# Reordering the operations of a pair on four engines, with carry and floor moved to ScalarE

## What is computed

```python
xn = _layernorm(x, axis=-1)
x = x + attn(xn, ...) + ffn(xn, ...)
...
# ffn: six layers (DEPTH = 6, HEADS = 16, DIM_HEAD = 64, WINDOW = 32)
for i in range(DEPTH):
    x = attn_layer(shift_tokens(x), Wqkv[i], ...) + x
    x = ffn_layer(shift_tokens(x), ...) + x
...
# attn_layer
q = l2norm(q) * qs
k = l2norm(k) * ksc
q = q * cos * scale + rotate_half(q) * sin * scale
k = k * cos * inv + rotate_half(k) * sin * inv
out = local_attention(q, k, v)   # each window of 32 sees itself and the window before
return out @ Wo
...
# ffn_layer
xn = (x - mu) / jnp.sqrt(var + 1e-05) * g + bln
a, gate = jnp.split(xn @ W1 + b1, 2, -1)
return a * jax.nn.gelu(gate, approximate=False) @ W2 + b2
```

## Time and profile before

| what | value |
|---|---|
| runs before | 3851.44, 3864.42, 3864.74 us, median 3864.42 |
| profiled execution | 3854.79 us, its span 3853.0 us |
| granted TensorE clock, mean | 0.984 |
| TensorE busy | 3672.5 us (95%) |
| VectorE busy | 3196.5 us (83%) |
| ScalarE busy | 2919.4 us (76%) |
| GpSimd busy | 3063.6 us (80%) |

### The profile page before, as it was taken

One profiled execution on the slowest core, in us unless ns is written; L12 is line 12 of the kernel. 1 busy time (PEld: TensorE's weight loads), 2 busy tenths in 40 slices (PEclk: granted clock), 3 DMA queues, 4 the chain that ended last, 5 costly groups with the idle time before them and its releaser, 6 DMA issues. The chain is left out here.

```text
span 3853.0 us, 176449 instructions
## 1 busy us (share of the span) xinstructions
PE 3672.5 (95%) x66944; PEld 2523.9 (66%) x66944; DVE 3196.5 (83%) x6391; ACT 2919.4 (76%) x6003; POOL 3063.6 (80%) x3927
## 2 busy tenths in 40 slices
PE   4999997899999999999999999999999999999997
PEld 2344443567777777777777777777777777777775
DVE  6888884788888888888888888888888888888885
ACT  6466666677777887778777777787778777778874
POOL 5111112989999999999999999999999999999993
PEclk7899999999999999999999999999999999999998
DMA  3433221222222322223222232222232222222222
GB/s 95 61 37 39 39 26 48 79 66 63 64 62 73 83 65 65 65 65 94 65 65 64 63 91 63 64 65 65 71 89 65 65 62 64 73 63 65 65 66 57
DMA packets 179255, 250.64 MB, mean 65 GB/s; under 512 B 46902, under 2 KB 69940, under 8 KB 178228
## 3 DMA queue, kind: packets, MB, share of 16 engines
q1 hardware_dynamic: 179124, 248.92, 26.7%
HBM read 39.07 MB, written 8.39 MB: 12 GB/s over the span
## 5 line engine op out<-in xcount | busy, mean ns | idle before, releaser
L1135 PE MATMUL w_ring<-shared,w_xs 128*128 (+1 forms) x2304 | 1157.3, 605 | 10.0 <-ACT w_xs L1325 4.7
L1540 POOL TENSOR_TENSOR w_qr<-w_raw,w_tc 128x512 f32<-128x512 f32 x384 | 489.0, 1273 | 146.4 <-PE w_ring L1155 138.3
L1554 POOL TENSOR_TENSOR w_qr<-w_qr,w_qrot 128x512 f32<-128x512 f32 x384 | 575.6, 1499 | 0.0
L1135 PEld LDWEIGHTS w_ring<-shared,w_xs 128*128 128x128 f32 x2304 | 378.8, 191 | 176.9 <-issue 143.6
L1547 POOL TENSOR_TENSOR w_qrot<-w_raw,w_tc 128x512 f32<-128x512 f32 x384 | 486.3, 1277 | 0.0
L1217 PEld LDWEIGHTS w_ring<-w_pts,w_vw 64*64 64x64 f32 x24576 | 377.0, 135 | 94.2 <-issue 94.1
L693 ACT ACTIVATE a_probs<-a_wide 128x512 f32<-128x512 f32 (+1 forms) x608 | 314.4, 581 | 156.5 <-PE a_wide L601 154.0
L733 POOL TENSOR_SCALAR_AFFINE_SELECT a_probs<-a_probs 128x512 f32<-128x512 f32 x128 | 81.6, 638 | 441.6 <-ACT a_probs L693 441.6
L764 DVE TENSOR_REDUCE a_row_max<-a_ring 128x1 f32<-128x512 f32 (+3 forms) x608 | 360.9, 654 | 85.2 <-PE a_ring L580 60.4
L1332 ACT ACTIVATE w_ksq<-w_ring 128x512 f32<-128x512 f32 x384 | 229.4, 598 | 251.6 <-PE w_ring L1135 251.6
L1217 PE MATMUL w_ring<-w_pts,w_vw 64*64 64x32 f32 x24576 | 398.6, 220 | 5.2 <-issue 3.5
(11 more groups left out here) (171 smaller groups left out, 8631.0 us busy)
## 6 DMA issues: line engine op xcount, KB each, us to landing
w_vw<-w_v SPq DMA_DIRECT2D x1152, 128.0 KB, 2.3
w_vw<-w_v SPq DMA_DIRECT2D x768, 64.0 KB, 2.0
shared<-in_L_ffn_Wqkv SPq DMA_DIRECT2D x6, 1536.0 KB, 6.0
shared<-q_parts SPq DMA_DIRECT2D x108, 64.0 KB
shared<-k_parts SPq DMA_DIRECT2D x108, 64.0 KB
q_parts<-ap_parts SPq DMA_DIRECT2D x8, 384.0 KB, 4.4
k_parts<-ap_parts SPq DMA_DIRECT2D x8, 384.0 KB, 5.0
shared<-in_L_ffn_Wo SPq DMA_DIRECT2D x12, 256.0 KB, 3.2
```

The source lines that it names most:

```text
L1135: nc.tensor.matmul(bank(what, i, u)[:], xs[u][:], rhs, start=True, stop=True).then_inc(done, 1)
L1540: nc.gpsimd.tensor_tensor(by_head(qr[i][:]), by_head(raw[i][:]), wide(table(u, Q_COS)), ALU.mult).then_inc(q_straight[i], 1)
L1554: nc.gpsimd.tensor_tensor(qr[i][:], qr[i][:], qrot[i][:], ALU.add).then_inc(q_added[i], 1)
```

## The change

The order of the calls in `body` is another one on TensorE, ScalarE, GpSimd and VectorE, and `USES` follows TensorE's. Beside that, `carry` goes from GpSimd to ScalarE, and so does the addition of the floor 1e-24 to the clamped sums (it was the first instruction of `refine`). `LAG` is 5 instead of 6. Some waits are added on GpSimd for its own operations, and a semaphore in `prepare` is replaced by one that was there.

```diff
-        LAG = 6
+        LAG = 5
...
             def body(pair):        # TensorE
                 scores(pair - 3, 0)
-                ffn_out(pair - 5)
                 turn_p(pair - 4, 1, 1)
-                turn_p(pair - 4, 1, 0)
                 project(pair - 2, 0, "q", 1)
+                project(pair - 3, 1, "v", 1)
+                turn_p(pair - 4, 1, 0)
+                ffn_out(pair - 5)
                 project(pair - 2, 0, "k", 1)
                 values(pair - 4, 1)
                 project(pair - 3, 1, "v", 0)
-                project(pair - 3, 1, "v", 1)
...
                 project_out(pair - 4, 1)
+                turn_k(pair - 3, 1, 0)
                 turn_q(pair - 3, 1, 0)
+                project(pair - 2, 1, "q", 0)
                 project(pair - 2, 0, "v", 0)
-                turn_k(pair - 3, 1, 0)
-                project(pair - 2, 1, "q", 0)
                 ffn_turn(pair - 4)
                 turn_p(pair - 3, 0, 1)
                 scores(pair - 3, 1)
                 project(pair - 2, 1, "q", 1)
                 turn_p(pair - 3, 0, 0)
+                project(pair - 2, 0, "v", 1)
                 project(pair - 2, 1, "k", 1)
-                project(pair - 2, 0, "v", 1)
                 ffn_back(pair - 4)
                 values(pair - 3, 0)
                 turn_k(pair - 2, 0, 1)
                 project(pair - 2, 1, "k", 0)
+                ffn_hidden(pair - 4, 1)
                 ffn_hidden(pair - 4, 0)
-                ffn_hidden(pair - 4, 1)
+                turn_q(pair - 2, 0, 0)
+                ffn_hidden(pair - 4, 2)
+                turn_k(pair - 2, 0, 0)
                 turn_q(pair - 2, 0, 1)
-                turn_q(pair - 2, 0, 0)
-                turn_k(pair - 2, 0, 0)
+                project(pair - 1, 0, "q", 0)
                 project_out(pair - 3, 0)
-                ffn_hidden(pair - 4, 2)
-                project(pair - 1, 0, "q", 0)
...
                 nc.scalar.activation(lnv[:], over[:], ACT.Ln, bias=tiny[:, 0:1]).then_inc(logged, 1)
+                nc.scalar.activation(ssc[:], over[:], ACT.Identity, bias=tiny[:, 0:1]).then_inc(floored, 1)
...
+            def carry(r, u):       # on ScalarE
...
+                factor = keep[:, bass.ds(r % PAIRS_B, 1)] if u == 0 else 1.0
+                nc.scalar.activation(kt[u][:, :, 0:BAND], kt[1 - u][:, :, P:KEYS], ACT.Copy, scale=factor).then_inc(carried, 1)
...
             def body(pair):        # ScalarE
-                copy_v(pair - 2, 1, 0)
-                copy_v(pair - 2, 1, 1)
-                store_c(pair - 3, 1, 1)
-                square_k(pair - 1, 0, 0)
-                store_kt(pair - 2, 1, 1)
-                store_qt(pair - 2, 1, 1)
                 build_xs(pair - 1, 1)
+                store_c(pair - 3, 1, 1)
+                store_c(pair - 3, 1, 0)
+                square_k(pair - 1, 0, 0)
+                copy_v(pair - 2, 1, 0)
+                store_kt(pair - 2, 1, 1)
                 clamp(pair - 1, 0)
-                factor_log(pair - 1, 0)
+                store_kt(pair - 2, 1, 0)
                 build_xf(pair - 3)
+                factor_log(pair - 1, 0)
+                store_qt(pair - 2, 1, 1)
                 factor_seed(pair - 1, 0)
-                store_kt(pair - 2, 1, 0)
                 store_qt(pair - 2, 1, 0)
...
+                store_p(pair - 2, 0, 0)
                 square_q(pair - 1, 1, 1)
-                store_p(pair - 2, 0, 0)
                 square_k(pair - 1, 1, 1)
                 copy_q(pair - 1, 1, 1)
                 exps(pair - 2, 1, 0)
+                exps(pair - 2, 1, 1)
                 scale_xn(pair - 3)
+                carry(pair - 1, 0)
+                store_c(pair - 2, 0, 0)
                 copy_v(pair - 1, 0, 1)
-                exps(pair - 2, 1, 1)
-                choose_rows(pair - 1)
-                build_xs(pair, 0)
-                square_k(pair - 1, 1, 0)
-                store_c(pair - 2, 0, 0)
-                store_c(pair - 2, 0, 1)
                 store_kt(pair - 1, 0, 1)
-                gelu(pair - 3, 0)
+                square_k(pair - 1, 1, 0)
                 gelu(pair - 3, 1)
-                store_kt(pair - 1, 0, 0)
-                store_qt(pair - 1, 0, 1)
+                store_c(pair - 2, 0, 1)
+                gelu(pair - 3, 0)
                 store_qt(pair - 1, 0, 0)
+                build_xs(pair, 0)
                 gelu(pair - 3, 2)
+                store_kt(pair - 1, 0, 0)
                 square_q(pair, 0, 0)
+                store_qt(pair - 1, 0, 1)
                 clamp(pair - 1, 1)
...
```

## The result

The changed kernel took 3975.5 us (median; 3972.3 to 3980.5), beside 3861.2 us of the kernel before on the same chip: a ratio of 1.030, interval 1.028 to 1.033. It is slower by 114 us; the forecast was 74 us (3935 for 3861).

The account below looks back on a forecast made before the run. The prediction took TensorE's stream as the bound: 0.97 us lost waiting for tokens minus 0.18 gained at the division, 0.79 us per pair, +76 us over 96 pairs, median put at 3935 us; range 3840 to 4000.

Parts of the forecast that it names:

- What bounds the kernel: All six layers run on TensorE's stream; a change gains or loses only TensorE's waits; a pair takes 32.58 us mid-run.
- The division: VectorE's division ends 0.54 us after the GpSimd operation it meets; the turn of the probabilities comes earlier, gaining 0.18 us per pair.
- The stall: TensorE's first projection of the next pair waits for build_xs(pair,0), late on ScalarE; cost 0.97 us per pair, bounds 0.75 to 1.3.
- TensorE's own 7.56 us: TensorE's work from the end of the projection of k to the next pair's first projection, summed to 7.56 us.
- TensorE's load 0.06 later: Last step of ScalarE's chain: TensorE's load follows build_xs's end at 8.37 by 0.06 us, at 8.43 us.
- this candidate: store_qt(0,1) before the scores, ready at 11.6, wanted at 11.9 us; would take over if ScalarE lost 0.3 us more.
- Parts that cost nothing: Semaphore, LAG 5, GpSimd waits, moved ffn_out, normalise_x and window DMAs: together -0.1 to +0.2 us per pair.
- The sum: 0.97 - 0.18 = 0.79 us per pair, 32.58 to 33.37; over 96 pairs +76 us.
- the forecast's own case: Whole kernel slower, at 3890 to 3970 us; chance 0.64.
- the third rival: The token wait breeds others: scores wait for store_qt(0,1), late seed holds refine and turns; 3979 to 4037 us, chance 0.09.
- The first two rivals: First: build_xs in time, faster, 3802 to 3847 us, chance 0.16. Second: waits nearly cancel, 3864 to 3884 us, chance 0.11.
- The rule on table loads: Skill page's 2.66 us per ScalarE table switch, 1.38 us drain included, would add 125 us; forecast used the rows instead.

Follow-up runs that it names:

- the run without a wait there: copy_v(pair-1,0,1) put back ahead of two store_c on ScalarE, against the reordered kernel at 3891.4 us; 3849.8 us, ratio 0.9978.
- the run with that wait last: Kernel before with build_xs(pair,0) late (3895.2 us), its first projection now waiting for bank and weights first, tokens last; 3883.3 us, ratio 1.0073.
- the early copy: Changed kernel with build_xs(pair,0) alone moved right behind exps(pair-2,1,1) on ScalarE, 13 steps earlier; 3971.7 us, ratio 1.0301.
- the late copy in the order of before: Kernel before with build_xs(pair,0) alone moved between store_qt(pair-1,0,0) and gelu(pair-3,2); 3895.2 us, ratio 1.0098.

## Why the prediction was right in direction and short in size

**What bounds the kernel: right.** TensorE's stream, its waits, and the pair's length decide. The experiments moved the time by what they did to TensorE's waits and, with the window DMAs, to the length of its score products; in the order of before, moving carry and floor between two other engines moved nothing.

**The division: mechanism right, size 0.08 of 0.18.** VectorE and GpSimd in the kernel after:

```profile
2023.59 1.08 DVE L1714 TENSOR_TENSOR w_p<-w_p,w_rinv 128x512 f32<-128x512 f32 x1
```

```profile
2022.85 1.28 POOL L1554 TENSOR_TENSOR w_qr<-w_raw,w_tc 128x512 f32<-128x512 f32 x1 [1.40 <-PE w_ring L1155]
```

The division ended at 2024.67, again 0.54 us behind the end of the GpSimd operation that it met (2024.13). That operation lay 0.1 us later than assumed, so the turn came 4.97 us behind project_out, not 4.87 (before 5.05). With 0.05 us behind it, the stretch gained 0.13, and the longer scores took 0.14 again.

**The stall: there, at the place named, and too small.** The term was 0.97 us: 0.87 ahead of `q0` and 0.10 for the drained array. Measured are 1.32 and 0.09. From the end of the projection of k (2030.37) the sum had 8.37 us to the end of build_xs; it ended at 2038.80, 8.43. Link by link: square_k at 0.20 as forecast, carry 0.40 for 0.38, square_k(1,0) and the table load 0.66 + 1.29 for 0.62 + 1.30. TensorE's own 7.56 us was right to the hundredth, as the run without a wait there shows. What failed is the last step, "TensorE's load 0.06 later": 0.06 is what the division's wait had in the trace of before; here the matmul came 0.45 us behind the copy (8.88). That is 0.39 us, 37 us over the pairs, and the chain's 0.06 makes up the rest of 0.45. Of the 0.39, the run with that wait last shows 0.13 to be instructions that stood behind it; the rest is open. The forecast took the wait for the only thing on the path; the early copy shows that the stores behind it in ScalarE's order hold the scores 0.03 us earlier or later just the same. The text saw this candidate ("ready at 11.6, wanted at 11.9"; it ended at 11.67, and the products began at 11.94) and was right that it did not add to the stall, but it means that the loss is the chain's and not the copy's.

**"Parts that cost nothing", bounded by +0.2: wrong, and on both sides.** Not seen: build_xs(pair-1,1) with its register instructions ahead of two store_c, +0.30 by project_out's start and 22 us by the run that moved it; the window DMAs, of which the text asked whether their reader would wait (it didn't) but not what runs beside them, +0.14; project_out(.,0), 0.09 longer. In TensorE's favour: -0.50 between `q0` and the scores, beside the 0.09 of the drained array that is counted above, and -0.05 because ffn_out no longer stands right behind the scores (1.30 us for 1.40, while the turn that stands there now takes 0.50 for 0.44). The -0.50 is of the kind that halved the late copy in the order of before. With a remainder of -0.01 these items add up to -0.03 us.

**The sum.** Forecast 0.79 us per pair, measured 1.25. The missing 0.46 is 0.44 of the stall (1.41 for 0.97), 0.05 of the division (0.13 for 0.18) and -0.03 of the rest. That the rest is so small is luck: +0.53 and -0.55 us that were not foreseen. 96 x 0.46 = 44 us, against 40 us between forecast (3935) and result (3975.5), which lies just above the forecast's own case (3890 to 3970) and below the third rival's (3979 to 4037). The first two rivals did not come: build_xs ended at 8.43 us, past the 7.5 us at which the first began. The third came near in size and half in mechanism. refine did wait for its late seed (34.9 us in 94 times from 1600 to 3200 us, at most 0.6; in the kernel before not once), but no turn waited for GpSimd. And the products began 0.27 us behind the end of store_qt(0,1), where in the run with the early copy, in which the scores did wait for it, they began 0.25 behind: the scores were at the edge of that wait, not in it.

**The rule on table loads.** The rows of the kernel after say the same as those of before: gelu began 1.29 us behind the start of the load, and the load 0.02 us behind the end of the operation ahead of it. The Trainium skill, page "ScalarE: Activation LUTs", section "What ACT_TABLE_LOAD costs", gives some 2.66 us for a switch, drain included; the forecast did not use it, and by it, an estimate, the chain would have ended 1.4 us later than it did: the trace disagrees, and it decides. The same section's 93 ns for a per-partition pointer operand agrees nearly with the trace: the median carry with one took 512 ns, without 431 ns, 81 ns less.

## What to carry to other kernels

When operations of an in-order engine are moved, follow every one of its results to its reader and every bank it frees to the next user, not only the one that becomes late first: here taking away one wait gave nothing that can be told twice, because the next stood right behind it, and 42 us the third time; and a swap that took one away cost 13 us, because it gave another matmul a bank that came free later. Do not take the distance from producer to consumer of one wait for that of another: register instructions and other waits behind a wait come on top. Put the wait that ends last at the very end (12 us here), and try to have what computes addresses ahead of it, which no run here tested by itself. Ask of a transfer that moves not only who reads it, but which products run beside it, and ask it for the rare pair too: here the order that helped some 90 pairs lost half of its gain in five, one per layer.

## What the runs showed of the hardware

- A matmul behind a blocking wait started 0.44 to 0.45 us after the end of its input, 0.31 us with that wait placed last. Matmuls that waited for a bank started 0.14 to 0.15 us after its reader (turn_q behind store_c in the kernel after, ffn_hidden behind copy_v and behind add_k in two of the runs), and the turn behind the division in the trace of before 0.06 us.
- ScalarE's copy of the tokens, with 207 ns of register instructions behind its waits, started 0.64 us behind the projection it waited for, as the first call of the body and behind two stores alike; square_k, without such instructions, started 0.20 us behind its own.
- The 128 small score products, with full clock in all, took 1.38 to 1.41 us with the DMA engines quiet and 1.53 to 1.75 us with them busy for 56 to 66% of the time (129 to 150 GB/s). The runs don't tell which shared resource it is, nor why 1.75 us went with the lower rate.
- VectorE's 128x512 division meeting a GpSimd operation ended 0.54 us after it, in both kernels. Two later ones of the kernel after (from 2038.84, 1.67 us, and from 2041.28, 0.92 us) ended 0.55 us after theirs, and GpSimd's 128x512 operations beside them took 1.73 us instead of 1.27: each holds the other up.
